# Moving float splits, activation tables and an attention's last pieces in a four-layer attention and expert kernel

## What is computed

```python
x = x + L0_attention(layernorm(x), ctx)     # 16 heads, additive mask, biases
x = x + L0_experts(layernorm(x))            # 8 experts, top 2, relu squared
x = x + L1_attention(layernorm(x), ctx)     # 16 heads
x = x + L1_experts(layernorm(x))            # 8 experts, top 1
x = x + L2_attention(layernorm(x), ctx)     # 16 heads, scores clipped to -5..5, key mask
x = x + L2_dense(layernorm(x))              # silu(x w1) * (x w2), gelu(h1), gelu(h2), w3
x = x + L3_attention(layernorm(x), ctx)     # 8 heads
x = x + L3_experts(layernorm(x))            # top 1, second norm, sigmoid mix
```

## Time and profile before

| | us |
|---|---|
| median of three runs | 918.51 |
| profiled execution | 924.34 |
| its span (first to last instruction) | 922.6 |
| TensorE busy | 773.5 (84%) |
| DVE busy | 557.1 (60%) |
| ScalarE busy | 505.5 (55%) |
| POOL busy | 277.7 (30%) |
| mean granted TensorE clock | 0.937 |

### The profile page before, as it was taken

One profiled execution on the slowest core, in us unless ns is written; L12 is line 12 of the kernel. 1 busy time (PEld: TensorE's weight loads), 2 busy tenths in 40 slices (PEclk: granted clock), 3 DMA queues, 4 the chain that ended last, 5 costly groups with the idle time before them and its releaser, 6 DMA issues.

```text
span 922.6 us, 15702 instructions
## 1 busy us (share of the span) xinstructions
PE 773.5 (84%) x4631; PEld 612.8 (66%) x4631; DVE 557.1 (60%) x1967; ACT 505.5 (55%) x1662; POOL 277.7 (30%) x326
## 2 busy tenths in 40 slices
PE   3997978788887989989995999889999977757497
PEld 1575756657665667778973777738668855547497
DVE  4756646645447879655547887652232058984775
ACT  1876757235545987845644645464434255542275
POOL 4200023335550435433531434200010012342255
PEclk9999989869999999999997999999999998996599
DMA  7854694213225200002226920000000050000121
GB/s 228 221 174 183 155 217 119 71 48 85 82 63 218 70 1 13 10 17 68 60 78 193 210 55 1 1 0 1 1 1 0 1 183 1 1 12 13 45 69 48
DMA packets 35955, 69.57 MB, mean 75 GB/s; under 512 B 7120, under 2 KB 25808, under 8 KB 32032
## 3 DMA queue, kind: packets, MB, share of 16 engines
q1 hardware_dynamic: 30384, 57.98, 22.5%
q0 software_dynamic: 4768, 9.91, 3.1%
q10 hardware_dynamic: 720, 0.68, 0.2%
HBM read 58.45 MB, written 37.67 MB: 104 GB/s over the span
## 4 chain that ended last, share of the span: by engine, by line
PE 48%; DVE 22%; ACT 11%; issue 9%; POOL 6%; another core or an unknown queue 2%; DMA 1%; SPq 1%; DVEq 0%; POOLq 0%; ACTq 0%
PE bank L1156 9%; PE bank L1028 6%; PE bank L997 5%; PE bank L1131 4%; PE bank L956 3%; PE bank L1026 3%; PE bank L1011 3%; DVE s_xn L1309 3%; POOL out L2012 3%; ACT s_S L1820 2%; PE bank L1110 2%; PE bank L1104 2%; DVE s_peak L1346 2%; DVE s_total L1357 2%; POOL xs_L L2005 2%
## 5 line engine op out<-in xcount | busy, mean ns | idle before, releaser
L997 PE MATMUL bank<-s_A,s_xTq 128*128 128x462 f32 (+1 forms) x352 | 153.6, 528 | 23.8 <-DVE s_S L1343 11.6
L1978 POOL TENSOR_TENSOR s_S<-s_S,s_inv 128x462 f32<-128x462 f32 (+2 forms) x123 | 100.7, 837 | 167.8 <-DVE s_inv L1360 166.3
L1011 PE MATMUL bank<-s_ident,s_S 128*128 128x128 f32 (+2 forms) x560 | 91.0, 283 | 33.2 <-POOL s_S L1978 21.2
L1011 PEld LDWEIGHTS bank<-s_ident,s_S 128*128 128x128 f32 (+2 forms) x560 | 66.7, 143 | 76.8 <-POOL s_S L1978 35.7
L1843 ACT ACTIVATE s_PT<-bank 128x384 f32<-128x384 f32 (+1 forms) x176 | 81.7, 472 | 46.2 <-PE bank L1011 42.7
L1028 PE MATMUL bank<-s_VW,s_PT 128*128 128x128 f32 (+2 forms) x800 | 104.6, 288 | 1.9 <-DVE s_x L1390 1.9
L1028 PEld LDWEIGHTS bank<-s_VW,s_PT 128*128 128x128 f32 (+2 forms) x800 | 100.7, 204 | 6.7 <-DVE s_x L1390 3.4
L2005 POOL DMA_INDIRECT xs_L<-s_xn,s_sli x64 | 62.0, 969 | 115.1 <-DVE s_sli L1467 76.1
L997 PEld LDWEIGHTS bank<-s_A,s_xTq 128*128 128x128 f32 x352 | 57.6, 201 | 41.5 <-issue 13.5
L1811 ACT ACTIVATE s_S<-s_S 128x462 f32<-128x462 f32 (+1 forms) x80 | 45.3, 566 | 62.4 <-DVE s_S L1338 32.6
L1820 ACT ACTIVATE s_S<-s_S,s_peak 128x77 f32<-128x77 f32 x256 | 67.8, 351 | 7.6 <-DVE s_peak L1346 7.1
(11 more groups left out here) (235 smaller groups left out, 1672.1 us busy)
## 6 DMA issues: line engine op xcount, KB each, us to landing
xs_L<-xs_L SPq DMA_DIRECT2D x24, 1122.0 KB, 30.6
s_xe<-xs_L SPq DMA_DIRECT2D x85, 66.0 KB
s_moe<-in_L_w SPq DMA_DIRECT2D x2, 2048.0 KB, 10.6
s_moe<-in_L_w SPq DMA_DIRECT2D x8, 512.0 KB, 7.6
s_yb<-ys_L SPq DMA_DIRECT2D x12, 256.0 KB, 3.2
s_arena<-in_L_w SPq DMA_DIRECT2D x2, 1024.0 KB, 6.1
s_arena<-in_L_h SPq DMA_DIRECT2D x2, 1024.0 KB, 8.7
s_b2bc<-in_L_b SPq DMA_DIRECT2D x2, 512.0 KB, 24.5
```

Of the source, the lines that this page charges most:

```text
L997: mm(bank[b][:, 0:(h1 - h0) * KEYS], xTq_of(L, n)[:, i % 4, :], A[:, n, h0 * KEYS:h1 * KEYS], start=True, stop=True).then_inc(scores.up(L, ...
L1011: w = turn(bank[b][0:m, P * (t - t0):P * (t - t0) + P], S[s][:, P * t:P * t + m], ident)
L1978: p.tensor_tensor(val, val, rep(inv[s][:, h0:h1], KEYS, 2), ALU.mult).then_inc(normed.up(L, i, k), 1)
```

## The change

- `ON_DVE[2]` is 12: in layer 2 the exponentials of heads 12 to 15 are taken one by one with their sums, and DVE's second reduce covers six heads.
- The side queue of splits is gone. Splits 0 to 3 stand behind the four `up` pieces of the second 512 tokens, splits 4 to 7 behind the first four h1 pieces.
- `tables` stands ahead of the last eight `down` pieces.
- `finish` of layer 3 has an order of its own: the four sends of group 1 stand behind the last tile's `norm`, group 2 is gated before the last tiles' output, and group 3 is placed and sent before group 4's second norm.
- `finish` of layer 0 puts three pieces of keys, not four, ahead of group 4's choice.
- `sched` takes fewer steps: the running sum is one reduce over overlapping windows instead of three adds, and the first row and expert of a block come from one comparison. `jt[1]` gets a ninth column, written once in `tok`; `cnt`, two of `cs` and one of `jt` are gone.

```diff
-ON_DVE = (0, 6, 16, 6)
+ON_DVE = (0, 6, 12, 6)
...
+        sent1 = [p for p in sides["after1"] if p[0] == "send"] if L == 3 else []
+        sides["after1"] = [p for p in sides["after1"] if p not in sent1]
         drain()
...
-                ("xt", "r", 0, 4), *steps("route", 4, 0), ("sigm", 0, 4), *keyed(4),
+                ("xt", "r", 0, 4), *steps("route", 4, 0), ("sigm", 0, 4), *keyed(3),
...
+        elif L == 3:
+            choice, rest = upto(("route", 3, 2, 6), rest)
+            rows2 = [p for p in choice + rest if p[0] in ("ln", "own")]
+            choice = [p for p in choice if p[0] == "route"]
+            rest = [p for p in rest if p[0] in ("route", "weigh")]
+            now(("norm", 3, z, 0), *(("T", 3, z - 1, q) for q in nq), ("norm", 3, z, 1), *sent1, ("xt", "r", 3, 2),
+                ("O", 3, z - 2))
+            add(z - 2)
+            now(*rows2[:2], *norm("r", 3, 1), *(("T", 3, z, q) for q in nq), *norm("r", 3, 2), *rows2[2:3], *choice[:4],
+                ("O", 3, z - 1), *norm("r", 3, 3, 4, 5, 6, 7), *choice[4:], ("O", 3, z), ("xt", "r", 3, 3))
+            add(z - 1)
+            now(*rows2[3:])
+            add(z)
+            now(*norm("x", 3, 1), ("own", 3, 0), *norm("r", 4, 1, 2), *norm("x", 3, 2), *steps("route", 3, 0, 1),
+                *rest[:1], *norm("r", 4, 3, 4, 5, 6, 7), ("xt", "r", 3, 4), *rest[1:], *late, *steps("route", 4, 0),
+                *steps("route", 3, 2, 3, 4, 5, 6, 9), *steps("route", 4, 1), *steps("route", 3, 7),
+                *steps("route", 4, 2, 3), *norm("x", 3, 3, 4, 5, 7), ("own", 3, 1), *steps("weigh", 3, 0),
+                *steps("route", 4, 4, 5, 6), ("sched", 3, 0), *steps("route", 3, 10, 11), *norm("x", 4, 1), ("own", 4, 0),
+                *norm("x", 4, 2), *steps("weigh", 3, 1, 2), *steps("route", 3, 12), *sends(3, 3),
+                *steps("route", 4, 9), ("sched", 3, 1), ("sched", 3, 2), ("sched", 3, 3),
+                *norm("x", 4, 3, 4, 5, 7), ("own", 4, 1), *steps("weigh", 4, 0, 1, 2), *steps("route", 4, 10, 11, 12),
+                *sends(3, 4), *(("sched", 3, st) for st in range(4, 7)))
+            return
...
-    side("split", [("split", n) for n in range(8)])
     attention(2)
...
             put("up", g, o)
+            if g:
+                put("split", o)
...
                     put("mid", h, gg, o)
+                    if h == gg == 0:
+                        put("split", 4 + o)
...
+        if g:
+            put("tables")
         for gg in (g, g + 1):
             for t in range(4):
                 put("down", 4 * gg + t)
...
-    put("tables")
     attention(3)
...
+    def windows(ap, first, n):
+
+        return bass.AP(ap.tensor, ap.offset + first, [list(ap.ap[0]), [1, n], [1, n]])
...
+                v.tensor_scalar(jt[1][:, :, 8], iotaj, float(P), None, ALU.mult)
...
                 if h0 < ON_DVE[L]:
-                    v.tensor_reduce(total[s][:, h0:h1], S[s][:, h0 * KEYS:h1 * KEYS].rearrange(
+                    h2 = min(h1, ON_DVE[L])
+                    v.tensor_reduce(total[s][:, h0:h2], S[s][:, h0 * KEYS:h2 * KEYS].rearrange(
...
-                    for n, e in enumerate((1, 2, 4)):
-                        again()
-                        v.tensor_tensor(cs[n + 1][:, 8:16], cs[n][:, 8:16], cs[n][:, 8 - e:16 - e],
-                                        ALU.add).then_inc(own.up(), 1)
+                    again()
+                    v.tensor_reduce(cs[1][:, 0:8], windows(cs[0], 1, 8), AX, ALU.add)
+                    v.tensor_scalar(tlf, cs[0][:, 8:16], -float(P), float(EROWS), ALU.mult,
+                                    ALU.add).then_inc(own.up(), 1)
                 elif st == 4:
                     again()
-                    v.tensor_tensor(a, rep(ij, 8, 2), rep(first, nbk, 1), ALU.is_ge)
-                    v.tensor_tensor(c, rep(ij, 8, 2), rep(cum, nbk, 1), ALU.is_lt)
-                    v.tensor_scalar(tlf, first, -128.0, float(-SPARE), ALU.mult, ALU.add).then_inc(own.up(), 1)
+                    v.tensor_tensor(past, rep(iotaj[:, 0:nbk], 8, 2), rep(cs[1][:, 0:8], nbk, 1),
+                                    ALU.is_ge).then_inc(own.up(), 1)
                     again()
-                    v.tensor_tensor(d, a, c, ALU.mult)
-                    v.tensor_tensor(cnt, tlf, ebase, ALU.add).then_inc(own.up(), 1)
+                    v.tensor_tensor(part[:, :, 0:8], past, rep(tlf, nbk, 1), ALU.mult).then_inc(own.up(), 1)
                     again()
-                    v.scalar_tensor_tensor(c, rep(ij, 8, 2), 128.0, rep(cnt, nbk, 1), ALU.mult,
-                                           ALU.add).then_inc(own.up(), 1)
-                    again()
-                    v.tensor_tensor(a, c, d, ALU.mult).then_inc(own.up(), 1)
-                    again()
-                    v.tensor_reduce(jf[1][:, 0:nbk], a, AX, ALU.add).then_inc(own.up(), 1)
+                    v.tensor_reduce(jf[1][:, 0:nbk], part, AX, ALU.add).then_inc(own.up(), 1)
...
                 if L == 2 or h0 < ON_DVE[L]:
                     act.wait_ge(*(moved if L == 2 else shifted).at(L, i, k))
-                    a(S[s][:, c0:c1], S[s][:, c0:c1], ACT.Exp).then_inc(probs.up(L, i, k), 1)
+                    if h0 < ON_DVE[L]:
+                        w = a(S[s][:, c0:c1], S[s][:, c0:c1], ACT.Exp)
+                    else:
+                        for h in range(h0, h1):
+                            val = S[s][:, h * KEYS:h * KEYS + KEYS]
+                            w = a(val, val, ACT.Exp, accum_out=total[s][:, h:h + 1])
+                    w.then_inc(probs.up(L, i, k), 1)
```

More of the change, by code:

```diff
@@ L640, in body @@
     ysf = put("ysf", [P, 2, 4])
-    cnt = put("cnt", [P, 8])
     cmp16 = put("cmp16", [P, 8, 16])
-    cs = [put(f"cs{i}", [P, 16]) for i in range(4)]
-    jt = [put(f"jt{i}", [P, 39, 8]) for i in range(3)]
+    cs = [put(f"cs{i}", [P, 16]) for i in range(2)]
+    jt = [put(f"jt{i}", [P, 39, w]) for i, w in enumerate((8, 9))]
     jf = [put(f"jf{i}", [P, 39]) for i in range(2)]
@@ L1500, in vector_program @@
                 L, st = at
[L1501 to L1504, removed]
+                nbk = BLOCKS[L]
+                past, part = jt[0][:, 0:nbk, :], jt[1][:, 0:nbk, :]
                 if st == 0:
@@ L1510, in vector_program @@
                 elif st == 2:
+                    dve.wait_ge(*filled.at())
                     again()
@@ L1513, in vector_program @@
                 elif st == 3:
-                    dve.wait_ge(*filled.at())
-                    for n, e in enumerate((1, 2, 4)):
-                        again()
-                        v.tensor_tensor(cs[n + 1][:, 8:16], cs[n][:, 8:16], cs[n][:, 8 - e:16 - e],
-                                        ALU.add).then_inc(own.up(), 1)
+                    again()
+                    v.tensor_reduce(cs[1][:, 0:8], windows(cs[0], 1, 8), AX, ALU.add)
+                    v.tensor_scalar(tlf, cs[0][:, 8:16], -float(P), float(EROWS), ALU.mult,
+                                    ALU.add).then_inc(own.up(), 1)
@@ L1531, in vector_program @@
-                    v.tensor_tensor(a, c, d, ALU.mult).then_inc(own.up(), 1)
-                    again()
-                    v.tensor_reduce(jf[1][:, 0:nbk], a, AX, ALU.add).then_inc(own.up(), 1)
+                    v.tensor_reduce(jf[1][:, 0:nbk], part, AX, ALU.add).then_inc(own.up(), 1)
                 elif st == 5:
                     again()
-                    v.tensor_scalar_add(jr[:, 0:nbk], jf[1][:, 0:nbk], float(SPARE)).then_inc(block_row.up(L), 1)
-                    v.tensor_tensor(a, d, rep(iota8, nbk, 1), ALU.mult).then_inc(own.up(), 1)
@@ L1538, in vector_program @@
-                    again()
-                    v.tensor_reduce(jf[0][:, 0:nbk], a, AX, ALU.add).then_inc(own.up(), 1)
+                    v.tensor_scalar(jr[:, 0:nbk], jf[1][:, 0:nbk], float(SPARE), None,
+                                    ALU.min).then_inc(block_row.up(L), 1)
+                    v.tensor_reduce(jf[0][:, 0:nbk], past, AX, ALU.add).then_inc(own.up(), 1)
                 else:
                     again()
-                    v.tensor_copy(je[:, 0:nbk], jf[0][:, 0:nbk]).then_inc(block_expert.up(L), 1)
+                    v.tensor_scalar(je[:, 0:nbk], jf[0][:, 0:nbk], float(NE - 1), None,
+                                    ALU.min).then_inc(block_expert.up(L), 1)
```

## The result

The changed kernel takes 906.38 us (median of 4 runs, 903.93 to 908.35) against 918.86 for the kernel before (median of 4): 12.5 us less by the medians, ratio 0.985 with an interval of 0.982 to 0.987, which is 11.6 to 16.5 us. The forecast was 905.6, in a range of 901.5 to 912.0. The profiled executions differ by more (spans of 922.6 and 902.2, 20.4), and the first half of the program varies from one execution to the next: 7.6 of the 20.4 lie ahead of the third attention, where the change touches only the schedules, a fold and one small operation. So I read the stages, not the spans.

What follows compares the result with a forecast made beforehand. No engine fills the span; gains must come from the third attention's head, the joint before the fourth and its end. Terms -8.0 - 1.0 + 2.8 - 1.8 - 4.0 - 1.1 + 0.2 = -12.9 from 918.5 give 905.6 us, range 901.5 to 912.

Steps and rivals of the forecast that it cites:

- Splits out of the head: Head of the third attention: seven splits on DVE's path and their waits for ScalarE go, -8.0 us (ends -4.5 and -9).
- Sums on ScalarE: Third attention's last four heads: ScalarE's extra 0.8 a tile is covered, DVE's shorter reduces give -1.0 us (+1.5 to -3).
- the stall's clock: Third attention: after TensorE stood 2.25 us, matmuls ran at clock 0.50; a shorter stall may spare some, within the -1.0.
- rival C: Third attention: ScalarE sets the tile period, 1.8 a tile, 27 us, 933; chance 0.05 slower, 0.03 without change.
- Splits in the dense stage: Gating phase and first h1 pieces: moved splits delay TensorE by +2.8 us (ends +2.0 and +4.4).
- the longer ring: Gating phase, DVE product, ScalarE rounding, DVE remainder: a split delays each next product about 0.62, the eighth by 1.86 us.
- the stand: First h1 piece, dense stage: after nine matmuls TensorE waits 1.6 us, from 621.9 to 623.5, for the fourth split.
- Rival B: Dense stage: the clock falls to half rate after TensorE's new wait, 1.6 us more, 907.2; chance 0.22.
- Table load: Before the fourth attention: one load under the down matmuls replaces two in the norm, -1.8 us (ends -1.3 and -2.6).
- D: Rival: the table loads reappear before the fourth attention, 907.4; chance 0.02.
- End of the fourth attention: POOL's sends go behind the last norm and group 3's placement comes earlier: -4.0 us (ends -2.0 and -5.5).
- Schedule and fold: Routed layers' shorter schedule: nothing, covered by sends; one fold fewer before the first layer's last counting: -1.1 us.

Runs made afterwards that it cites:

- the first group of experiments: Group in which the changed kernel, unaltered, was run again beside the kernel before on one chip: 878.13 us, ratio 0.983.

## Why the prediction was right

The mechanism was right, and the terms lie near what was measured by stage:

- **Splits out of the head**: -8.0 predicted, -9.0 measured (24.32 to 15.29). The step's 9.1 and its "I allow 1 us of new waits" were about right: with the splits alone moved the second reciprocal comes 8.4 earlier, and DVE has two new waits, 0.67 and 0.20, for TensorE's scores. What the sum lacked is the other 0.6, behind the reciprocal: before, TensorE ran at half rate there up to 510.1, and with the splits gone at full rate (granted 0.74 and 1.00 from the reciprocal to the first output matmul). That half rate costs this much there, the changed kernel's two profiles show: 15.86 with 3.5 us of it in the head, 15.29 without. This was the largest miss.
- **Sums on ScalarE**: -1.0 predicted, -0.5 measured. The tiles' period stayed 5.40 and ScalarE's added time was covered. The part credited to the stall's clock was chance: the same stand is followed by half rate in one run and not in the next. The pairs in place start 0.25 apart, though the two records of a pair are 0.25 and 0.19 long; so they overlap, and rival C, whose 27 us rested on pairs that do not, is out.
- **Splits in the dense stage**: +2.8 predicted, +2.9 measured, and made as the step has it: 1.06 for the longer ring ahead of the first h1 piece (1.24 in the step), 1.8 for the stand (1.6). Rival B is out: in none of the nine profiles that have the stand is half rate granted between the first h1 matmul and the last. B's price of 1.6 had no working; the rows it points at give 3.69 - 2.40 = 1.3. Where half rate did come near, it was in the ring ahead of it (gating of 18.12 and 18.25 in two runs), 1.0 each.
- **Table load**: -1.8 predicted, -2.1 measured. D is out.
- **End of the fourth attention**: -4.0 predicted, -4.8 measured. "-3.7 there" for the last norm on POOL was 3.5, of which the end kept 3.2. The new order adds 1.6. The five last sends begin 4.8 earlier (102.9 to 98.1 from the stage's start), just above the 3.0 to 4.7 of the step's estimate, and all of it came through to the end.
- **Schedule and fold**: 0 predicted and no change seen; -1.1 predicted for the fold, -0.5 measured: on the path, but priced at half rate, which ends inside the folds in the profiles compared here. The +0.2 for the small operation at the start was undone together with the schedule and is not told apart.

The measured terms make -9.0 - 0.5 + 2.9 - 2.1 - 4.8 - 0.5 = -14.0. The medians say -12.5 in the first result and -14.6 in the first group of experiments. So that the forecast of -12.9 lies 0.4 from the first result is in part luck: against the stages head, tail and tables were underrated by 2.1 and sums and fold overrated by 1.1, and the medians of four executions leave the saving anywhere from 11.6 to 16.5. Why the first half varies is not explained.

## What to carry to other kernels

Price work that two engines share by both engines' queues: a split cost 0.66 of DVE in the groups and 1.1 to 1.4 where DVE had to wait for ScalarE's half. In one run it was free where TensorE ran without a gap on results that the two engines take in turn, as in the folds, and it was not where an engine merely idled in front of its next wait, as in the tiles. A price read off the chain holds for the clock it was read at: look at the granted clock of that row first.

## What the runs showed of the hardware that I had not expected

The same program took 906.38 us in the first result and 878.13 among the experiments, 28 less; the two profiled executions differ by 26, and nearly all of that lies in two stages: the first attention (146.8 against 156.2 from first score to first fold) and the first layer's experts (53.7 against 69.1 from the first block to the next joint). In the experts' stage, waits of the weight loads, first profile and second:

```profile
PEld bank L1136 <- issue: 9.4, 13, 0.8
```

```profile
PEld bank L1136 <- issue: 0.8, 2, 0.6
```

"Issue" is time in which the engine waited for nothing that the profile shows. The stages from the third attention on agree between the two to 0.1 where the granted clock does. The four chips of the experiments agree within 1.2 us on the kernel before, so chips need not differ like this; whether the first result's chip does, or something else was otherwise then, is not shown, and what held the weight loads up is open.

The granted clock followed the order of the work in one place and chance in another: the stall in the middle of the third attention was followed by half rate in four of twelve profiles, and the head's 13.7 us of half rate came in both profiles with the splits in it.
